# A selective scan beside a summed-factor layer: VectorE multiplies by C directly behind the scan

## The reference, cut to what matters

```python
def step(state, inp):
    d, b, c, u = inp
    dA = jnp.exp(d[..., None] * A)
    state = state * dA + (d * u)[..., None] * b[:, None, :]
    y = jnp.einsum('bdn,bn->bd', state, c)
    return (state, y)
...
y = y + D[None, :, None] * x
y = y * silu(z)                    # z = _layernorm(x)
...
x = x + y                          # y with its last two axes swapped
mixed = jnp.einsum('btd,rde->bte', _layernorm(x), factors) / math.sqrt(8) + bias
return x + mixed
```

## Time and profile before

| | |
|---|---|
| median of 3 runs | 516.74 us (516.27 to 518.4) |
| profiled execution | 520.92 us |
| its span, first to last instruction | 519.1 us |
| VectorE busy | 478.5 us, 92% |
| GpSimd busy | 453.7 us, 87% |
| TensorE busy | 420.7 us, 81%, mean granted clock 0.936 |
| ScalarE busy | 343.2 us, 66% |

### The profile page before, as it was taken

How to read it: one execution, slowest core, us unless ns; L and a number is a source line. 1 busy time by engine, 2 the same in 40 slices (tenths; PEclk the granted TensorE clock), 3 DMA queues, 4 the chain that set the end, 5 groups by cost and what they waited for, 6 DMA issues and landing times.

```text
span 519.1 us, 3987 instructions
## 1 busy us (share of the span) xinstructions
PE 420.7 (81%) x984; PEld 173.3 (33%) x992; DVE 478.5 (92%) x384; ACT 343.2 (66%) x608; POOL 453.7 (87%) x233
## 2 busy tenths in 40 slices
PE   8644868598788957989898898879878698888897
PEld 5111323233323322434333343324333243333343
DVE  4688999999999999999999999998999898978985
ACT  2477574686559877798778875788688574733421
POOL 1026999999999999999999999998998699999934
PEclk9875989989899889999899899989999899998999
DMA  5979645442985000010692000000692000000002
GB/s 178 266 201 394 237 81 121 81 81 53 266 291 206 0 0 1 13 48 1 226 412 75 0 21 1 21 0 0 200 412 83 0 20 21 21 20 21 0 1 81
DMA packets 17615, 53.96 MB, mean 104 GB/s; under 512 B 2724, under 2 KB 2724, under 8 KB 16568
## 3 DMA queue, kind: packets, MB, share of 16 engines
q1 hardware_dynamic: 16440, 45.31, 24.3%
q0 software_dynamic: 1152, 8.39, 7.9%
HBM read 49.24 MB, written 4.46 MB: 103 GB/s over the span
## 4 chain that ended last, share of the span: by engine, by line
DVE 39%; PE 23%; issue 18%; POOL 12%; ACT 4%; DMA 4%; DVEq 0%; SPq 0%; POOLq 0%; ACTq 0%
DVE dA L832 18%; PE y L437 11%; DVE h L832 7%; POOL h L960 7%; DVE h L838 7%; POOL h L953 3%; PE work L366 3%; DMA b_rep<-bc_scratch 2%; DVE acc L773 2%; PE work L407 2%; PE work L430 2%; ACT dA L651 2%; DVE work L813 1%; PE work L415 1%; PE work L358 1%
## 5 line engine op out<-in xcount | busy, mean ns | idle before, releaser
L960 POOL TENSOR_TENSOR h<-b_rep,dtu 128x1024 f32<-128x1024 f32 x127 | 304.1, 2439 | 11.4 <-DMA b_rep<-bc_scratch 11.1
L437 PE MATMUL y<-h,ident 128*128 128x512 f32 x512 | 257.5, 640 | 55.8 <-DVE h L838 44.6
L651 ACT ACTIVATE dA<-dt,a_neg 128x512 f32<-128x512 f32 x256 | 165.8, 679 | 110.7 <-DVE h L838 79.2
L832 DVE TENSOR_TENSOR_SCAN dA<-dA,h 128x1024 f32<-128x1024 f32 x80 | 182.8, 2285 | 2.6 <-ACT dA L651 1.8
L437 PEld LDWEIGHTS y<-h,ident 128*128 128x128 f32 x512 | 97.8, 201 | 199.4 <-issue 108.1
L953 POOL TENSOR_TENSOR h<-h,c_rep 128x1024 f32<-128x1024 f32 x48 | 115.6, 2409 | 5.5 <-DVE h L832 5.4
L832 DVE TENSOR_TENSOR_SCAN h<-dA,h 128x1024 f32<-128x1024 f32 x48 | 109.5, 2280 | 6.9 <-ACT dA L651 4.1
L838 DVE TENSOR_TENSOR h<-dA,c_rep 128x1024 f32<-128x1024 f32 x80 | 97.3, 1216 | 1.7 <-DMA c_rep<-bc_scratch 0.8
L358 PE MATMUL work<-ctx_sb,w_in 128*128 128x512 f32 x60 | 31.9, 668 | 10.0 <-DVE x L852 9.0
L773 DVE SCALAR_TENSOR_TENSOR acc<-work,chan,acc 128x511 f32<-128x511 f32 (+2 forms) x45 | 32.4, 729 | 1.2 <-ACT acc L538 1.0
L430 PE MATMUL work<-fsum,xnT 128*128 128x512 f32 x64 | 28.8, 592 | 0.0
(11 more groups left out here) (117 smaller groups left out, 375.7 us busy)
## 6 DMA issues: line engine op xcount, KB each, us to landing
b_rep<-bc_scratch SPq DMA_DIRECT2D x32, 512.0 KB, 8.5
c_rep<-bc_scratch SPq DMA_DIRECT2D x32, 512.0 KB, 8.6
fsum<-factors POOLq DMA_DIRECT2D x8, 1024.0 KB, 8.1
x<-x SPq DMA_DIRECT2D x4, 1024.0 KB, 10.2
out<-x SPq DMA_DIRECT2D x16, 256.0 KB, 2.0
ctx_sb<-ctxT SPq DMA_DIRECT2D x3, 512.0 KB, 5.0
ctx_sb<-ctxT SPq DMA_DIRECT2D x2, 256.0 KB, 4.3
w_in<-w_inT SPq DMA_DIRECT2D x2, 256.0 KB, 4.6
```

Source lines behind the costliest of these rows:

```text
L437: mm = pe.matmul(y[:], ident[:], h[:, (s * PAIRS + j) % H_RING, i, :], start=False, stop=(j == SUM_ORDER[-1] and i == 1))
L651: act.activation(dA[:, j % 2, i, :], dt[:, k % 2, :], ACT.Exp, scale=a_neg[:, k, 2 * j + i:2 * j + i + 1]).then_inc(exp_done, 1)
L832: dve.tensor_tensor_scan(pair if j in POOL_C else decay, decay, pair, 0.0, ALU.mult, ALU.add).then_inc(scanned, 1)
L960: pool.tensor_tensor(h[:, (s * PAIRS + j) % H_RING], b_rep[:, j], dtu[:, k % 2, :].unsqueeze(1).to_broadcast([P, 2, L]), ALU.mult).then_in ...
```

## The change

In VectorE's `step` the call of `times_c` moves from the end of a pair to the place directly behind the scan. The smaller piece of work of that pair then stands behind the product.

```diff
                 for j in range(PAIRS):
                     scan(s, j)
+                    if j not in POOL_C:
+                        times_c(b, s, j)
 
                     if j == 0 and s > 0 and nv - 1 < STEPS:
                         conv_part(work0, nv - 1, 3)
...
                         conv_part(work0, nv, 1)
                     if j == 7 and is_c:
                         conv_part(work0, nv, 2)
-                    if j not in POOL_C:
-                        times_c(b, s, j)
```

## The result

The changed kernel is slower. Its first 4 executions took 522.07 to 527.0 us, median 524.15, against 517.4 for the kernel before, a ratio of 1.0135 with a 95% interval of 1.008 to 1.0189. Taken again beside three experiments it came to 1.0114 (1.0085 to 1.0144), 5.9 us. The forecast was +2.0, its range ended at 521.6. The ratios here leave out executions more than 1.5% above the fastest of their kernel, so where a kernel's own spread is that wide, the median says more than the ratio.

A forecast was written before the change was run, and what follows sets the result against it. VectorE was taken to bound the kernel; 53 pairs at 0.13 us made 6.9 us, of which waits swallow about 4.9 net, so +2.0: the median goes from 516.74 to 518.7 us, range 515.2 to 521.6.

The forecast's parts named there:

- What bounds, and the cost between neighbours: Whole loop: VectorE sets the pace; a product directly behind its scan costs 0.13 us per pair, 53 pairs, 6.9 us.
- Rival 1: The order is free on VectorE, or something hides the 0.12 us: 515.5 us, strong form 513.7; chance 0.14.
- Waits at (4, 4) and (6, 0): At (4, 4) the wait of 0.61 us goes, leaving the scan 1.21 late; at (6, 0) 0.41 goes, leaving 1.58.
- is 1.97 late: Scan at (8, 4) 1.97 us late, through TensorE's layer and the gates, like the last product of step 7.
- End of step 10: Three waits there swallow about 2.3 us of 3.01, as TensorE is not later; delay 0.7 at (11, 0).
- rival 2: Step 10 doesn't swallow, x projection starting after 348.4: delay 3 at (11, 0), 4.4 at (11, 5), 521.0 us; chance 0.21.
- (11, 5): Scan there: the later residual sum adds 1.27 us and neighbours 0.13 to a delay of 0.7, making 2.1.
- the layer for the `raw_final` at 437.40 ends 2.9 later: Step 13: later residual sum holds TensorE, layer 2.9 us late; less the product of 1.13, 1.8 at (13, 6).
- the bounds: Limits on what no row shows, TensorE's clock included: -3 to +6.9 us, or +7.5 with half of the late sum.
- Step 12: It keeps the delay of 2.1 us; the 0.26 of its moved pairs lies in the wait of 0.94.
- From (13, 6) to (15, 0): Delay 1.8 us at (13, 6), 2.45 at (14, 0), 1.4 at (15, 0), then 2.0 at the end.
- The range: Expected median 515.2 to 521.6 us; the forecast's own range was +0.9 to +3.2, chance 0.50.

The follow-up runs named there:

- memset run: Changed kernel with a 128x1 memset between scan and product in pairs 1, 3 and 7 of every step; span 521.3 us, a single execution.
- step 11 kernel: Kernel before with the residual sum behind the product at (11, 3) alone; ratio 1.0021, median 522.96 against 518.37 us.
- convolution run: Kernel before with only the convolution parts behind the product, 20 pairs in steps 0 to 9; ratio 1.0017, median 520.49 us.
- run of the residual sum: Kernel before with only the residual sum of the odd steps behind the product, 8 pairs; ratio 1.0057, median 521.27 us.

## Why the prediction was wrong

- **What bounds, and the cost between neighbours: right.** 4.06 us for the pair with the gate, 0.60 us for step 9 against the 0.52 forecast. The term was sized a little small: 0.14 to 0.15 per pair instead of 0.13. With 0.28 that stand at (1, 1) already this is 0.7 us at (8, 1). Rival 1 is out. The sentence quoted from the Trainium skill (VectorE: DVE Perf Modes, "The DRAIN you can't avoid") was read too widely: the same section says that a next op which is not held starts earlier. The trace fits that sentence: in the kernel before, every other kind of instruction starts about 2.20 us behind a scan, and only the product, which waits for it, 2.32.
- **Waits at (4, 4) and (6, 0): right** to 0.15 us.
- **"is 1.97 late" at (8, 4): the first step that failed.** I let TensorE follow the last product of step 7 without delay. The later residual sum, 1.27 us at the input projection, I had left out here, and alone it would not have mattered: with TensorE's clock of before (0.68) the layer started 0.6 us less late than the scan at (8, 1), as forecast, in two profiles with this order. In the changed kernel the clock was 0.54 and the two pieces took 1.4 us more; with the 1.27 that left no gap, and the layer started 0.8 us later than the scan. Error 1.4 us.
- **End of step 10: the right amount, in part by luck.** From 5.35 to 3.05, 2.3 swallowed, as forecast. But the waits there, 1.50 us of them at (11, 0), I took for waits behind TensorE in any execution. They were long because TensorE's sum and x projection ran at low clock in the profiled one, which the 2.99 us for four matmuls in the earlier trace rows already showed; the early product brings full clock. The x projection also began 2.4 us later than before, at 348.48, where I had 346.1; that is just past the 348.4 that I had set as the mark of rival 2. Its delays of 3 at (11, 0) and 4.4 at (11, 5) nearly came true too, but not its mechanism, since the waits did go: VectorE came 5.35 us late itself, for what had happened in step 7.
- **(11, 5): right**, +1.26 against 1.4.
- **"the layer for the `raw_final` at 437.40 ends 2.9 later": the second step that failed.** I had TensorE at full clock behind its longer gap; the sum behind the transposes took 3.57 instead of 1.98. Beyond the delay of the scan at (13, 5) the layer was 2.1 us late where the forecast had 0.55; in the memset run, at full clock, it was 0.4. Error 1.5 us. I had named the clock under the bounds, and given it nothing in the sum.
- **Step 12**, where I let the delay stand, added 0.35. From (13, 6) to (15, 0) the delay changed by -0.45 against -0.4, and from there to the end by +0.6, as forecast.
- **The range** ended at what VectorE could lose and left TensorE's clock out. Of the error of 4.05 us in the profile 2.9 are TensorE's clock in steps 7 and 13, 0.7 the neighbours and the start, and 0.35 step 12. The runs put 0.64% on the residual sum and 0.41% on the gate, the pieces that TensorE waits for, and nothing that can be told on the other 30 pairs.

Open: where the upper group of the step 11 kernel loses its 5 us was not seen, as both its profiles fell into the lower one. In its neighbour, moved in steps 11, 13 and 15, the upper profile was late by TensorE's clock at three places, but one of them lies ahead of the change. Why a late sum in step 11 makes slow stretches elsewhere more frequent is open.

## What to carry to other kernels

Put the piece that another engine waits for ahead of one that it doesn't, even if the latter frees a buffer: here the product freed `dA` for an engine with slack, and the gate and the residual sum were what TensorE stood for. The product directly behind its scan cost VectorE about 0.12 us, so independent work between the two is worth its place, though 30 such pairs (0.09%) could not be told in the time. When a forecast moves a start of TensorE, follow TensorE's own gap to the next layer, and price its clock behind a longer idle time as a term of the sum. And see what TensorE's clock was in the profile that a forecast starts from: a wait behind a stretch at the low level may not be there in the next execution.

## What the hardware showed beyond that

- A gap in front of TensorE's matmuls decides nothing by itself. At (10, 3) and (13, 3) together, over 20 profiles, full clock followed in all 12 cases with 0.35 to 1.48 us, and in 12 of 28 with 2.09 to 3.47 us. Full clock came behind 3.46 us at (10, 3) in the convolution run and behind 3.56 us at step 7 in the run of the residual sum; behind 3.36 to 3.47 us at (13, 3) all three profiles had the low level.
- One stretch of TensorE at the low level, at (13, 3), went with 0.95 us more delay at (13, 6) in the changed kernel and with 4.8 us more in the run of the residual sum, where dt projection and layer ran at it as well.
- In the kernel before six kinds of instruction start about 2.20 us behind a scan of 128x1024 (row 2.28), whatever they are: scan, gate, residual sum, softplus, convolution part, `raw_final`. The product that reads the scan starts at 2.32.
- A memset of 128x1 fits between a scan and the product that reads it without moving the product (2.30 to 2.34 us in 48 pairs with it and in 80 without).
